# Two cross-attentions in a six-stage kernel: products with values of the preceding batch directly behind the scores, all key and value units behind them

## The chip, the cores and the metric

The kernel runs on one core of a Trainium2 chip. The metric is the device time of one execution in microseconds (us). The median of three runs is 664.64 us (663.59 to 665.05). Names of engines: PE is TensorE (matrix products; PEld is its loading of weights), DVE is VectorE, ACT is ScalarE, POOL is GpSimd, SP is SyncE, which issues the DMAs here.

## The reference, cut to what matters

The input is `x` of 16 batches x 32 tokens x 256 channels, and a context of 16 batches x 512 keys x 256 channels. Six stages follow one another; each adds its result to `x` after a layer norm. Two of them are cross-attentions with 16 heads of 16 channels, and the change is in these:

```python
# stage 1 (L0), x = x + this; _qdq rounds to int8 steps
q = _qdq(layernorm(x)) @ _qdq(wq).T + bq
k, v = split(ctx @ wkv.T + bkv)
attn = softmax(einsum('bnhd,bmhd->bhnm', q, k) / sqrt(16))
out = _qdq(einsum('bhnm,bmhd->bnhd', attn, v)) @ _qdq(wp).T + bp
# stage 4 (L1), x = x + this
scores = where(attend, clip(q @ k / 4, -50, 50), -10000), clipped again
probs = softmax(scores); ctx = probs @ v
delta = layernorm(rs * (ctx @ Wo.T + bo)) * gamma + beta
```

Stages 2 and 5 are self-attentions, stages 3 and 6 feed-forward blocks; nothing in them changes.

## The kernel before, in words

There is no scheduler: each engine's program is written out by hand in its order, and engines wait for one another by semaphores. `xattn` (from L195) writes both cross-attentions, with `L0` true for the first stage. Both run over the 16 batches. What one batch b needs of PE:

- **Scores**: `scores_rows` in stage 1 (L426, 8 products in the program, queries on the partitions), `scores_cols` in stage 4 (L441, 16 products, keys on the partitions). Four banks of PSUM, `S`, take them.
- **Units** of keys and values (`unit_pe`): keys and values of a context batch are four units, two of keys (L388) and two of values (L396). They run some batches ahead of the scores that read them. `slot(b, k)` says which unit stands in which place of batch b: three places a batch, now and then a fourth in stage 1, two from batch 10 on in stage 4, none in the last batch. Units take the two banks `U` in turn; a unit waits until its bank's last unit, two before it, has been copied out. Even units are copied out by ACT (`unit_act`, L674 and L676), odd ones by DVE (`unit_dve`, L685 and L687).
- **Products with values** (`values`, L476, 64 products in the program): they are those of batch b-1, into one of the two banks `O`. In stage 4 they wait for all exponentials of batch b-1 (L561), in stage 1 for the transposed probabilities of b-1, for which the scores of b wait already (L418, L419).
- In stage 1 also **the turn** (`turn`, L451, 16 transposes): the probabilities of batch b are transposed for the next batch. Each quarter waits for its exponential (L694).

The softmax runs on DVE (a maximum in stage 1, L813; a clip in stage 4, L826) and ACT (exponentials, L694 and L700). `take_out` (L714) on ACT copies a batch's products with values out of bank `O`. At the first batch of each four it also waits until `turn_taken` (L493) on PE has read the buffer `oc`.

Every four batches make a tile of 128 tokens, and its end is spread over later batches: `turn_taken` transposes what was taken out (L493), `rows_ready` on DVE divides by the sums (and rounds in stage 1, L860 and L188 to L195), `turn_out` on PE transposes the result (L508 in stage 1, L510 in stage 4), `copy_out_cols` on ACT copies it to SBUF (L723), `out_rows` on PE multiplies by the output weight (L519), and DVE adds it up (L872, L877). `turn_out`, `copy_out_cols` and `out_rows` stand in batches 6, 10 and 14. In stage 4 `turn_taken` stands in batches 5, 9 and 13, in stage 1 in 4, 8 and 12.

What sets the order around the change are four functions: `batch_rows_pe` and `batch_rows_act` in stage 1, `batch_cols_pe` and `batch_cols_act` in stage 4. DVE's, POOL's and SP's programs are not touched. SP loads a context batch when the units of the batch three before it are done (three buffers, L312).

Of the kernel before, what the change touches and what calls it, by code (L numbers as in the profile page):

```python
# [197 lines left out]
def xattn(nc, e, take, sem, L0, d):  # L198
# [68 lines left out]
    TURN, READY, OUT, TAKE, NORM = 0, 1, 2, 2, 3  # L267
    n_weights = 6 if L0 else 10

    def tile_at(b, phase):  # L270

        t = b // 4 - 1
        return t if b % 4 == phase and 0 <= t < NT - 1 else None
# [92 lines left out]
    def slot(b, k):  # L366

        if not L0:
            u = FIRST + 3 * min(b, FULL) + 2 * max(b - FULL, 0) + k
            return None if k >= (3 if b < FULL else 2) or u >= 4 * NB else u  # L370
        u = FIRST + 3 * b + k + max(b - 1, 0) // 4
        return None if (k == 3 and (b % 4 or not b)) or u >= 4 * NB else u

    def unit_pe(pe, u):

        if u is None:
            return
        b, i = u // 4, u % 4
        bank = U[i % 2]
        wait(pe, s_ev[i % 2], 2 * b + i // 2)  # L380
        if i == 0:
            if b == 0:
                pe.wait_ge(s_wk, 16)
            pe.wait_ge(ctx_in[b % CB], 16 * (b // CB + 1))
        x = ctxT[b % CB]
        if i < 2:
            for c in range(NC):
                last = nc.tensor.matmul(bank, wkv[:, c, i * P:(i + 1) * P], x[:, c, :],  # L388
                                        start=(c == 0), stop=(c == NC - 1))
        else:  # L390
            if u == 2:
                pe.wait_ge(s_kv_in, 32)
            for kk in range(2):
                k = 2 * (i - 2) + kk
                for c in range(NC):
                    last = nc.tensor.matmul(bank[:, kk * D:(kk + 1) * D], x[:, c, k * P:(k + 1) * P],  # L396
                                            wkv[:, c, D:2 * D], start=(c == 0), stop=(c == NC - 1))
        last.then_inc(s_unit, 1)
# [97 lines left out]
    def turn_out(pe, t):  # L496

        if t is None:
            return
        pe.wait_ge(s_or, t + 1)  # L500
        if BPT * t + 5 < NB:
            pe.wait_ge(s_o, BPT * t + 5)
        elif after and not L0:
            pe.wait_ge(e.s_yT_out, after.at + t)
        for c in range(NC):
            cols = slice(c * P, (c + 1) * P)
            if L0:
                last = nc.tensor.matmul(OUTB[:, cols], whole[:, t, cols], identb, start=True, stop=True)  # L508
            else:
                last = nc.tensor.transpose(OUTB[:, cols], orow[:, t, cols], e.ident)  # L510
        last.then_inc(s_orT, 1)
# [16 lines left out]
    def batch_rows_pe(pe, b):  # L528

        scores_rows(pe, b)  # L530
        turn_out(pe, tile_at(b, OUT))
        unit_pe(pe, slot(b, 0))
        if b:
            for g in range(G):
                values(pe, b - 1, g)
        out_rows(pe, tile_at(b, TAKE))
        unit_pe(pe, slot(b, 1))
        for g in range(G):
            turn(pe, b, g)
        if b < NB - 1:  # L540
            next_turn(pe, tile_at(b, NORM))
        unit_pe(pe, slot(b, 2))
        turn_taken(pe, tile_at(b, TURN))
        unit_pe(pe, slot(b, 3))

    def batch_cols_pe(pe, b):

        scores_cols(pe, b, 0), scores_cols(pe, b, 1)
        turn_out(pe, tile_at(b, OUT))
        unit_pe(pe, slot(b, 0))  # L550
        turn_taken(pe, tile_at(b - 1, TURN))
        unit_pe(pe, slot(b, 1))
        if b:
            all_values(pe, b - 1)
        out_rows(pe, tile_at(b, TAKE))
        unit_pe(pe, slot(b, 2))
        next_turn(pe, normed(b))
        unit_pe(pe, slot(b, 3))
# [172 lines left out]

    def batch_rows_act(act, b):

        copy_out_cols(act, tile_at(b, OUT))
        exp_rows(act, b, 0), exp_rows(act, b, 1)
        for u in own(b, 0, 0):
            unit_act(act, u)
        exp_rows(act, b, 2), exp_rows(act, b, 3)
        if b:
            take_out(act, b - 1)  # L740
        for u in own(b, 0, 1):
            unit_act(act, u)
        copy_pT_act(act, b, 0), copy_pT_act(act, b, 2)
        if b < NB - 1:
            next_cols(act, tile_at(b, NORM))
        for u in own(b, 0, 2, 3):
            unit_act(act, u)

    def batch_cols_act(act, b):

        copy_out_cols(act, tile_at(b, OUT))
        exp_cols(act, b, 0), exp_cols(act, b, 1)
        for u in own(b, 0, 0):
            unit_act(act, u)
        exp_cols(act, b, 2), exp_cols(act, b, 3)
        for u in own(b, 0, 1):
            unit_act(act, u)
        if b:
            take_out(act, b - 1)
        for u in own(b, 0, 2):  # L760
            unit_act(act, u)
        next_cols(act, normed(b))
        for u in own(b, 0, 3):
            unit_act(act, u)
# [1524 lines left out]
```

## Time and profile before

| | |
|---|---|
| median of 3 runs | 664.64 us (663.59 to 665.05) |
| profiled execution, its own time | 665.43 us |
| its span in the profile | 663.6 us |
| stage 1, batches 0 to 15 | 37.2 us to about 200 us |
| stage 4, batches 0 to 15 | 409.7 us to about 543 us |
| PE busy over the span | 637.4 us (96%) |
| DVE, ACT, POOL busy | 421.4, 274.5, 59.0 us |
| PE's granted clock | 1.00 throughout |

A timeline row gives the start in us from the span's start, the length of the group, the engine, the line, the operation, the shapes and how often; in brackets how long the engine had idled before it, and what ended that. PE's groups overlap a little in these rows, because the ends of products are modelled. The time that a group takes is therefore read from its start to the next group's start. In the trace a product of 32-bit numbers counts as two instructions, so that the 64 products of `values` are 128 there, each with a weight load.

### The profile page before, as it was taken

The page shows a single profiled execution, that of the slowest core. Times are in us where ns is not written, and L with a number is a line of the kernel's source. Part 1 is how long each engine was busy: PE and PEld are TensorE (multiplying, and loading weights), DVE is VectorE, ACT ScalarE, POOL GpSimd, SP SyncE. Part 2 cuts the span into 40 slices and gives each one's busy share as a digit, 9 for nine tenths or more (in the row PEclk, how much of TensorE's full clock was granted, in tenths as well). Part 3 has the DMA queues.
Part 4 walks back from the last instruction along what each step waited for, and adds up shares of the span by engine and source line. Part 5 has one row for each costly group of instructions (what it writes and reads, how often), then busy time and mean ns, then how long its engine had stood idle before and what let it go on. Part 6 is the DMA issues. An engine that isn't in the chain of part 4 may idle for free.

```text
span 663.6 us, 21569 instructions
## 1 busy us (share of the span) xinstructions
PE 637.4 (96%) x9568; PEld 427.7 (64%) x9570; DVE 421.4 (63%) x981; ACT 274.5 (41%) x502; POOL 59.0 (9%) x130
## 2 busy tenths in 40 slices
PE   9999999999988999999999999999999999999976
PEld 4666667567565566666666666777767775466754
DVE  2744468587765656555554773554888965787487
ACT  3454445445442233434333844544454454011134
POOL 1020000001001111011111003000010101000000
PEclk9999999999999999999999999999999999999999
DMA  7241111117005410001003612110182100000001
GB/s 241 65 171 63 35 34 55 44 35 224 2 3 202 149 34 26 16 27 33 2 2 89 210 52 64 34 67 34 60 260 97 67 4 1 3 3 2 3 1 33
DMA packets 28957, 42.25 MB, mean 64 GB/s; under 512 B 6080, under 2 KB 18880, under 8 KB 28352
## 3 DMA queue, kind: packets, MB, share of 16 engines
q1 hardware_dynamic: 28720, 40.60, 19.1%
q8 instruction: 76, 1.25, 0.8%
q10 hardware_dynamic: 144, 0.26, 0.1%
q14 instruction: 17, 0.14, 0.1%
HBM read 40.33 MB, written 0.52 MB: 62 GB/s over the span
## 4 chain that ended last, share of the span: by engine, by line
PE 83%; DVE 11%; issue 2%; ACT 2%; DMA 1%; POOL 0%; SPq 0%; DVEq 0%; ACTq 0%
PE psum L396 16%; PE psum L388 16%; PE psum L1146 7%; PE psum L476 6%; PE psum L441 5%; PE psum L451 4%; PE psum L1197 4%; PE psum L1152 4%; PE psum L1882 2%; PE psum L426 2%; PE psum L1861 2%; PE psum L1167 2%; PE psum L1842 1%; PE psum L1181 1%; DVE arena L1978 1%
## 5 line engine op out<-in xcount | busy, mean ns | idle before, releaser
L396 PE MATMUL psum<-arena 128*128 128x256 f32 x512 | 121.6, 384 | 0.1
L388 PE MATMUL psum<-arena 128*128 128x512 f32 x248 | 117.8, 602 | 0.0
L396 PEld LDWEIGHTS psum<-arena 128*128 128x128 f32 x512 | 93.9, 190 | 22.0 <-issue 9.0
L388 PEld LDWEIGHTS psum<-arena 128*128 128x128 f32 x248 | 43.4, 190 | 41.0 <-issue 39.2
L700 ACT ACTIVATE arena<-arena 128x512 f32<-128x512 f32 x64 | 47.8, 804 | 35.5 <-DVE arena L826 35.5
L694 ACT ACTIVATE arena<-psum,arena 128x512 f32<-128x512 f32 x64 | 40.2, 687 | 31.0 <-DVE arena L813 30.9
L1146 PE MATMUL psum<-y_cols,arena 128*128 128x512 f32 x112 | 52.9, 605 | 0.0
L476 PEld LDWEIGHTS psum<-arena 128*17 128x17 f32 x4096 | 38.5, 96 | 20.1 <-issue 13.0
L826 DVE TENSOR_SCALAR arena<-psum 128x512 f32<-128x512 f32 x64 | 39.7, 681 | 17.9 <-PE psum L441 17.9
L1249 ACT ACTIVATE arena<-psum 128x512 f32<-128x512 f32 x48 | 28.2, 597 | 48.2 <-PE psum L1146 30.9
L813 DVE TENSOR_REDUCE arena<-psum 128x1 f32<-128x512 f32 x64 | 39.7, 683 | 12.8 <-PE psum L426 12.5
L674 ACT ACTIVATE arena<-psum,arena 128x512 f32<-128x512 f32 x42 | 28.8, 685 | 42.5 <-PE psum L388 36.8
L476 PE MATMUL psum<-arena 128*17 128x32 f32 x4096 | 42.7, 197 | 3.0 <-issue 2.9
L676 ACT ACTIVATE arena<-psum 128x512 f32<-128x512 f32 x42 | 25.1, 598 | 41.2 <-PE psum L396 41.2
L1303 DVE TENSOR_REDUCE arena<-psum 128x8 f32<-128x256 f32 x16 | 6.8, 425 | 48.1 <-PE psum L1167 48.1
L441 PEld LDWEIGHTS psum<-arena 64*128 64x128 f32 x512 | 29.9, 188 | 6.6 <-issue 6.1
L326 POOL TENSOR_TENSOR arena<-arena,head_mask 128x64 f32<-128x64 f32 (+1 forms) x64 | 20.7, 349 | 147.2 <-PE psum L426 92.1
L441 PE MATMUL psum<-arena 64*128 64x128 f32 x512 | 32.9, 278 | 0.0
L451 PEld LDWEIGHTS psum<-ident,arena 128*128 128x128 f32 x256 | 28.8, 141 | 6.0 <-issue 3.5
L1146 PEld LDWEIGHTS psum<-y_cols,arena 128*128 128x128 f32 x112 | 20.1, 189 | 18.6 <-issue 17.8
L451 PE MATMUL psum<-ident,arena 128*128 128x128 f32 x256 | 30.8, 273 | 1.2 <-ACT arena L694 1.2
L1152 PE MATMUL psum<-arena,y_cols 128*128 128x256 f32 x128 | 31.9, 392 | 0.0
(249 smaller groups left out, 932.7 us busy)
## 6 DMA issues: line engine op xcount, KB each, us to landing
arena<-in_ctxT SPq DMA_DIRECT2D x31, 512.0 KB, 3.7
arena<-in_L_attn_Wv SPq DMA_DIRECT2D x1, 2048.0 KB, 8.3
arena<-in_L_attn_Wq SPq DMA_DIRECT2D x8, 256.0 KB, 3.0
arena<-in_L_attn_Wk SPq DMA_DIRECT2D x8, 256.0 KB, 3.6
arena<-in_L_attn_Wo SPq DMA_DIRECT2D x1, 2048.0 KB, 12.3
arena<-in_L_ffn_w_gating SPq DMA_DIRECT2D x1, 2048.0 KB, 7.8
arena<-in_wo_rows SPq DMA_DIRECT2D x2, 1024.0 KB, 5.1
arena<-in_wq_upT SPq DMA_DIRECT2D x2, 768.0 KB, 7.7
```

The source lines that it names most:

```text
L388: last = nc.tensor.matmul(bank, wkv[:, c, i * P:(i + 1) * P], x[:, c, :], start=(c == 0), stop=(c == NC - 1))
L396: last = nc.tensor.matmul(bank[:, kk * D:(kk + 1) * D], x[:, c, k * P:(k + 1) * P], wkv[:, c, D:2 * D], start=(c == 0), stop=(c == NC - 1))
L441: ins = nc.tensor.matmul(S[2 * kp + r][:, (2 * kk + h) * P:(2 * kk + h + 1) * P], kT[home(b)][a, h, k * P:(k + 1) * P], qbd[b % QBUFS][a, ...
L451: last = nc.tensor.transpose(S[g][:, k * P:(k + 1) * P], pr[g][:, k * P:(k + 1) * P], e.ident)
L476: last = nc.tensor.matmul(O[b % 2][j * SQ:j * SQ + VW, g * SQ:(g + 1) * SQ], va[home(b)][:, k, head, :], probs[:, j * SQ:(j + 1) * SQ], st ...
L674: ins = nc.scalar.activation(kT[home(b)][:, i, :], U[i % 2], ACT.Identity, bias=bk[:, i:i + 1])
L694: nc.scalar.activation(pr[g], S[g], ACT.Exp, bias=nmx[:, g:g + 1]).then_inc(s_exp, 1)
L700: nc.scalar.activation(pTk[b % 2][k], clip[k // 2][:, k % 2, :], ACT.Exp, bias=mb[:, b, k:k + 1], scale=m01[:, b, k:k + 1]).then_inc(s_exp, 1)
L813: nc.vector.tensor_reduce(nmx[:, g:g + 1], S[g], AX.X, ALU.max, negate=True).then_inc(s_mx, 1)
L826: nc.vector.tensor_scalar(dst, S[i].rearrange("p (a n) -> p a n", n=P), 50.0, -50.0, ALU.min, ALU.max)\
L1146: last = nc.tensor.matmul(bank, w[:, c, f], e.yT[:, c, :], start=(c == 0), stop=(c == NC - 1))
L1152: last = nc.tensor.matmul(bank[:, (t % 2) * 2 * DV:(t % 2 + 1) * 2 * DV], e.yT[:, c, t * P:(t + 1) * P], wv[:, c, p * 2 * DV:(p + 1) * 2 * ...
```

## The change: the diff, and what it moves

In both stages the products with values of batch b-1 move up on PE, directly behind the scores of batch b, ahead of `turn_out` and of all units of the batch. On ACT, `take_out` moves up to follow them, between the first two and the last two exponentials; `copy_out_cols` moves from the head of the batch to behind it; and the copy of the batch's first unit moves behind the last two exponentials. The first batch has no products with values, so its order on PE stays, but ACT's changes there too. No instruction is added or removed.

```diff
--- before.py
+++ after.py
@@ -528,11 +528,11 @@
     def batch_rows_pe(pe, b):
 
         scores_rows(pe, b)
-        turn_out(pe, tile_at(b, OUT))
-        unit_pe(pe, slot(b, 0))
         if b:
             for g in range(G):
                 values(pe, b - 1, g)
+        turn_out(pe, tile_at(b, OUT))
+        unit_pe(pe, slot(b, 0))
         out_rows(pe, tile_at(b, TAKE))
         unit_pe(pe, slot(b, 1))
         for g in range(G):
@@ -546,12 +546,12 @@
     def batch_cols_pe(pe, b):
 
         scores_cols(pe, b, 0), scores_cols(pe, b, 1)
+        if b:
+            all_values(pe, b - 1)
         turn_out(pe, tile_at(b, OUT))
         unit_pe(pe, slot(b, 0))
         turn_taken(pe, tile_at(b - 1, TURN))
         unit_pe(pe, slot(b, 1))
-        if b:
-            all_values(pe, b - 1)
         out_rows(pe, tile_at(b, TAKE))
         unit_pe(pe, slot(b, 2))
         next_turn(pe, normed(b))
@@ -731,13 +731,13 @@
 
     def batch_rows_act(act, b):
 
+        exp_rows(act, b, 0), exp_rows(act, b, 1)
+        if b:
+            take_out(act, b - 1)
         copy_out_cols(act, tile_at(b, OUT))
-        exp_rows(act, b, 0), exp_rows(act, b, 1)
+        exp_rows(act, b, 2), exp_rows(act, b, 3)
         for u in own(b, 0, 0):
             unit_act(act, u)
-        exp_rows(act, b, 2), exp_rows(act, b, 3)
-        if b:
-            take_out(act, b - 1)
         for u in own(b, 0, 1):
             unit_act(act, u)
         copy_pT_act(act, b, 0), copy_pT_act(act, b, 2)
@@ -748,15 +748,15 @@
 
     def batch_cols_act(act, b):
 
+        exp_cols(act, b, 0), exp_cols(act, b, 1)
+        if b:
+            take_out(act, b - 1)
         copy_out_cols(act, tile_at(b, OUT))
-        exp_cols(act, b, 0), exp_cols(act, b, 1)
+        exp_cols(act, b, 2), exp_cols(act, b, 3)
         for u in own(b, 0, 0):
             unit_act(act, u)
-        exp_cols(act, b, 2), exp_cols(act, b, 3)
         for u in own(b, 0, 1):
             unit_act(act, u)
-        if b:
-            take_out(act, b - 1)
         for u in own(b, 0, 2):
             unit_act(act, u)
         next_cols(act, normed(b))
```

PE, stage 1, from the scores of batch 5 (first row) over those of batch 6 (seventh row) to the middle of batch 6, before (L388 and L396 units, L476 products with values of the batch before, L451 the turn, L508 `turn_out`, L519 `out_rows`):

```order
L426 MATMUL psum<-arena 64x512 x8
L388 MATMUL psum<-arena 128x512 x2
L476 MATMUL psum<-arena 17x32 x64
L388 MATMUL psum<-arena 128x512 x2
L451 MATMUL psum<-ident,arena 128x128 x16
L396 MATMUL psum<-arena 128x256 x4
L426 MATMUL psum<-arena 64x512 x8
L508 MATMUL psum<-arena 128x128 x2
L396 MATMUL psum<-arena 128x256 x4
L476 MATMUL psum<-arena 17x32 x64
L519 MATMUL psum<-arena 128x256 x2
L388 MATMUL psum<-arena 128x512 x2
```

The same stretch in the changed kernel:

```order
L426 MATMUL psum<-arena 64x512 x8
L476 MATMUL psum<-arena 17x32 x64
L388 MATMUL psum<-arena 128x512 x4
L451 MATMUL psum<-ident,arena 128x128 x16
L396 MATMUL psum<-arena 128x256 x4
L426 MATMUL psum<-arena 64x512 x8
L476 MATMUL psum<-arena 17x32 x64
L508 MATMUL psum<-arena 128x128 x2
L396 MATMUL psum<-arena 128x256 x4
L519 MATMUL psum<-arena 128x256 x2
L388 MATMUL psum<-arena 128x512 x2
L451 MATMUL psum<-ident,arena 128x128 x16
```

L476 now stands behind L426 in both batches, the unit that stood between them has joined the next unit (a unit of keys is two of L388, a unit of values four of L396; L388 x4 is two units), and in batch 6 L508 has the products with values ahead of it.

ACT, stage 1, batch 10 before, from its first instruction (L723 `copy_out_cols`, L694 exponentials, L674 copy of a unit, L714 `take_out`, L706 copies of the turn):

```order
L723 ACTIVATE arena<-psum 128x256
L694 ACTIVATE arena<-psum,arena 128x512 x2
L674 ACTIVATE arena<-psum,arena 128x512
L694 ACTIVATE arena<-psum,arena 128x512 x2
L714 ACTIVATE arena<-psum 128x4x32
L706 ACTIVATE arena<-psum 128x512 x2
```

The same batch in the changed kernel:

```order
L694 ACTIVATE arena<-psum,arena 128x512 x2
L714 ACTIVATE arena<-psum 128x4x32
L723 ACTIVATE arena<-psum 128x256
L694 ACTIVATE arena<-psum,arena 128x512 x2
L674 ACTIVATE arena<-psum,arena 128x512
L706 ACTIVATE arena<-psum 128x512 x2
```

L723 has moved from the head to behind two exponentials and L714; L674 stands behind the last exponential.

ACT, stage 4, batch 0 before, with the head of batch 1 behind it (L700 exponentials, L674 and L676 copies of units):

```order
L700 ACT_TABLE_LOAD
L700 ACTIVATE arena<-arena 128x512 x2
L674 ACTIVATE arena<-psum,arena 128x512
L700 ACTIVATE arena<-arena 128x512 x2
L676 ACTIVATE arena<-psum 128x32x16
L700 ACTIVATE arena<-arena 128x512 x4
```

And in the changed kernel:

```order
L700 ACT_TABLE_LOAD
L700 ACTIVATE arena<-arena 128x512 x4
L674 ACTIVATE arena<-psum,arena 128x512
L676 ACTIVATE arena<-psum 128x32x16
L700 ACTIVATE arena<-arena 128x512 x2
L714 ACTIVATE arena<-psum 128x4x32
```

The copy of the first unit (L674) has moved behind all four exponentials, and in batch 1 L714 stands between them.

## Rows read from the trace of the kernel before

**Rows 1.** The page: busy time and count by engine; the queue that carries instructions.

```profile
PE 637.4 (96%) x9568; PEld 427.7 (64%) x9570; DVE 421.4 (63%) x981; ACT 274.5 (41%) x502; POOL 59.0 (9%) x130
...
q8 instruction: 76, 1.25, 0.8%
```

**Rows 2.** Busy time by stretch: start:end length, then each engine's busy time; clock, DMA share.

```profile
37.20:190.10 152.90, 150.53 (x2590) 100.27 (x2589) 100.05 (x194) 74.36 (x134) 8.81 (x31) 1.00 0.22 72
409.70:545.00 135.30, 134.99 (x2867) 99.72 (x2867) 96.66 (x190) 67.95 (x114) 15.72 (x38) 1.00 0.26 80
```

**Rows 3.** Timeline of PE, first stage, one batch: start, length, instructions; in brackets idle before.

```profile
64.54 1.11 PE L426 MATMUL psum<-arena 32*64 32x512 f32 x16
65.58 1.99 PE L388 MATMUL psum<-arena 128*128 128x512 f32 x4
67.50 1.32 PE L476 MATMUL psum<-arena 128*17 128x32 f32 x128
68.75 1.99 PE L396 MATMUL psum<-arena 128*128 128x256 f32 x8
```

**Rows 4.** Timeline of PE, fourth stage, one batch.

```profile
434.59 2.06 PE L441 MATMUL psum<-arena 64*128 64x128 f32 x32
436.58 1.98 PE L388 MATMUL psum<-arena 128*128 128x512 f32 x4
438.40 1.89 PE L396 MATMUL psum<-arena 128*128 128x256 f32 x8
440.22 1.32 PE L476 MATMUL psum<-arena 128*17 128x32 f32 x128
441.47 1.99 PE L396 MATMUL psum<-arena 128*128 128x256 f32 x8
443.39 0.83 PE L441 MATMUL psum<-arena 64*128 64x128 f32 x10
```

**Rows 5.** Timeline of PE, fourth stage, last batch.

```profile
536.29 2.06 PE L441 MATMUL psum<-arena 64*128 64x128 f32 x32
538.28 1.32 PE L476 MATMUL psum<-arena 128*17 128x32 f32 x128
539.52 0.66 PE L1796 MATMUL psum<-arena 128*128 128x64 f32 x4
```

**Rows 6.** Timeline of PE, first stage, where a token tile is taken.

```profile
98.59 0.28 PE L508 MATMUL psum<-arena 128*128 128x128 bf16 x2 [0.29 <-DVEq L862]
```

**Rows 7.** Timeline of PE and ACT, first stage, batch 10.

```profile
138.56 1.11 PE L426 MATMUL psum<-arena 32*64 32x512 f32 x16
...
140.28 0.38 ACT L723 ACTIVATE arena<-psum 128x256 bf16<-128x256 f32 x1 [3.19 <-PE psum L508]
...
141.69 1.29 ACT L694 ACTIVATE arena<-psum,arena 128x512 f32<-128x512 f32 x2 [1.02 <-DVE arena L813]
...
144.58 0.30 ACT L714 ACTIVATE arena<-psum 128x128 f32<-128x128 f32 x1
```

**Rows 8.** Timeline of ACT and PE, fourth stage, batch 0.

```profile
412.17 1.52 ACT L700 ACTIVATE arena<-arena 128x512 f32<-128x512 f32 x2 [0.51 <-DVE arena L826]
...
415.19 1.89 PE L396 MATMUL psum<-arena 128*128 128x256 f32 x8
```

**Rows 9.** Timeline of PE and ACT, fourth stage, batch 8.

```profile
480.05 2.06 PE L441 MATMUL psum<-arena 64*128 64x128 f32 x32
...
483.17 1.52 ACT L700 ACTIVATE arena<-arena 128x512 f32<-128x512 f32 x2 [4.62 <-DVE arena L826]
...
484.60 0.67 ACT L674 ACTIVATE arena<-psum,arena 128x512 f32<-128x512 f32 x1
```

**Rows 10.** Timeline of PE, idle times inside or behind products with values.

```profile
77.11 1.19 PE L476 MATMUL psum<-arena 128*17 128x32 f32 x112
79.79 0.31 PE L476 MATMUL psum<-arena 128*17 128x32 f32 x16 [1.50 <-issue]
...
194.29 1.53 PE L451 MATMUL psum<-ident,arena 128*128 128x128 f32 x12 [0.95 <-ACT arena L694]
```

## Prediction

> **What bounds the kernel now.** I read the page first. PE is busy 637.4 of 663.6 us [rows 1], and the chain that ended last runs over PE for most of the span. The table by stretch then says what idle time is left in the two cross-attentions: 152.90 less 150.53 us, so 2.4 us, in stage 1 (ending before its last batch), and 0.3 us in stage 4 [rows 2]. So the change can't gain by filling idle time. It can gain only if PE's own work takes less time in another order, and it loses by every wait that it brings. The granted clock is 1.00 in both stretches [rows 2], the higher of the two levels (2.4 GHz), and PE has no pause to lose it in, so I leave the clock out.
>
> **What an order costs PE.** The timeline of one batch, read from start to start, shows that the same work takes different times by its neighbours. In stage 4 the first unit of the batch takes 1.82 us (436.58 to 438.40), the second 1.82, the third 1.92 (441.47 to 443.39) [rows 4]. The first has the scores before it, the second the products with values behind it, the third has both kinds of neighbour. So a side on which a unit meets scores or products with values costs 0.10 us, and a bare unit is 1.72. Stage 1 agrees: its first unit stands between scores and products with values and takes 1.92 (65.58 to 67.50) [rows 3]. I call such a side a border. Products with values take 1.25 us between two units (440.22 to 441.47) [rows 4]. In the last batch of stage 4 no unit stands between: scores 1.99 (536.29 to 538.28), products 1.24 (538.28 to 539.52) [rows 5], the same as with units around. So where scores meet products with values directly, nothing is seen to be paid.
>
> **Part 1, fewer borders.** A full batch has four borders before (scores to unit, unit to products, products to unit, unit to scores) and two after (products to unit, unit to scores): 2 x 0.095 = 0.19 us less, taking 0.095 for the border between these roundings. Stage 1 has 11 such batches (1 to 14 without 6, 10, 14): 2.1 us. Stage 4 has 8 (1 to 5, 7 to 9): 1.5. Batch 6 and batches 10 to 14 of stage 4 have other neighbours (an output product behind the products with values, or scores directly behind them); they save one border or less, 0.5 us together. Sum 4.1 us. Bounds: from below 2.1, if scores meeting products cost a border that the last batch doesn't show; from above no more than the 4.1.
>
> **Part 2, the wait of `turn_out` in stage 1.** In batches 6, 10 and 14 PE idles 0.29 us ahead of L508 [rows 6], since DVE has not finished rounding. After the change 1.25 us of products stand ahead of it, so DVE is long done. With one border less in each, 3 x (0.29 + 0.10) = 1.2 us. Next late there is `out_rows`, priced in part 3. From below the gain is nothing, from above 1.2.
>
> **Part 3, what ACT is late with.** ACT has idle time on average (its busy times in [rows 2] are half the stretches), so the moved instructions cost nothing by themselves; the copies of units and of `turn_out` are now behind exponentials, and these wait for DVE. I laid each batch out with the start-to-start times above. In a full batch of stage 4 PE's third unit, in the bank of the first, starts 1.99 + 1.25 + 1.82 + 1.72 = 6.78 us behind the start of the scores. ACT copies that first unit in even batches.
> - Stage 4, batch 0, has no products with values, and PE's order there is unchanged: its third unit starts at 415.19, right behind the second. ACT's exponentials start at 412.17, late behind a table load. Two of them hold ACT 1.43 us (483.17 to 484.60), a copy lasts 0.67 [rows 8, 9]. All four exponentials and then the copy: 412.17 + 2.86 + 0.67 = 415.70. PE waits 0.5 us.
> - Stage 4, batch 8: DVE is behind, so the exponentials start 3.12 us after the scores [rows 9], and 0.19 later by this measure once batch 7 is shorter. 3.31 + 1.43 + 0.20 for `take_out` (its 0.30 [rows 7] overlaps its neighbours) + 1.43 + 0.67 = 7.04, against 6.78. PE waits 0.3 us. In the other even batches the exponentials start 0.6 us earlier and the copy is there with 0.3 to 0.5 us to spare.
> - Stage 1, batch 10: the maxima on DVE are late, because rounding and a unit's copy stand ahead of them; the exponentials start at 141.69, 3.13 us behind the scores at 138.56 [rows 7]. Before, `copy_out_cols` stood ahead of them (140.28). Now it follows two exponentials (1.29) and `take_out`: 141.69 + 1.20 + 0.20 + 0.38 = 143.5. `out_rows` on PE is due at 138.56 + 1.04 for the scores [rows 3] + 1.25 + 0.28 for L508 [rows 6] + 1.72 = 142.85. PE waits 0.7 us. In batches 6 and 14 the exponentials start 0.9 us sooner, and 0.2 us are to spare.
> - The last batch of stage 4 has `take_out` amid its exponentials, ahead of the last products: 0.1 us.
>
> Together 1.6 us. In batches 5, 9 and 13 of stage 4 `take_out` waits for `turn_taken`, which now comes 1.25 us later on PE; behind it queue the last two exponentials and a copy, which nobody needs before the next batch. DVE's order is unchanged; it gets the first unit 1.25 us later, copies it in 0.7 and has it ready 0.9 us before its bank is wanted. POOL and SP wait for scores and for units done, and these keep their rhythm; no DMA is issued in another order. Bounds of part 3: 0.5 us, if only batch 0 slips; about 4 us, if every even batch of stage 4 loses 0.3 and batches 6 and 14 do too.
>
> **Part 4, instructions that arrive late.** Two waits of PE can't be explained by any engine: 1.50 us inside the products with values from 78.30 on, and 0.95 us from 193.34 on, behind them (the exponential named was over by then) [rows 10]. A third like them stands at the end of stage 1. PE and its weight loads are 19,138 instructions, brought by 76 packets of 1.25 MB in sum [rows 1], so a packet brings about 250. The products with values are 256 of them in 1.25 us; a whole batch has some 350 to 400. So about every batch some packet has to come within a short time, and the second wait stands at the one place of stage 1 where products directly follow scores. That is the order that all batches now get: scores and products are 290 to 320 instructions in 2.3 to 3.2 us, where before a unit or two lay between. What that costs no row shows for the new order. From below: -1.5, if the wait at 78.30 goes; from above: four waits more at about 1.3, 5.2 us. I take one more wait net of what may go, 1.5 us, near the rows that are there.
>
> **Sum.** 4.1 + 1.2 - 1.6 - 1.5 = 2.2 us less than the profiled execution's own 665.43: 663.2. That execution lies 0.8 us above the median 664.64, so the forecast is 662.5 us, 0.33% less. What a measurement of this kernel can tell from no change is about 0.2%, 1.3 us.
>
> The Trainium skill, page "TensorEngine Tiling (Array Packing)", section "Tiling Modes", says that a change of tiling mode drains TensorE. The units use the whole array, scores and products with values two different tilings (the shapes 64*128 and 128*17 in the rows), so by the rule scores meeting products is a change of mode as well, and a batch goes from four changes to three, not to two. The row of the last batch speaks against a price for this one; by the rule it would have one, and that is the second rival.
>
> **The rivals.**
> 1. Better than the forecast: no new instruction waits, and the one at 78.30 goes. 4.1 + 1.2 - 1.6 + 1.5 = 5.2 us, so 659.4. For it: such waits are rare in the trace before, three in 30 batches. Against it: the denser order.
> 2. Scores to products costs a border. One border less per batch, not two: 28 x 0.095 = 2.7 us less gain, but no less loss. 662.5 + 2.7 less what rounding leaves = 665.1, no change. For it: every other meeting of kinds costs 0.10. Against it: 1.24 us in [rows 5].
> 3. ACT slips at every even batch of stage 4: part 3 at 4 us instead of 1.6. 664.9, no change. For it: the margins of 0.2 to 0.5 us are small against semaphore times, which I have not counted one by one.
> 4. Slower: late instruction packets. The mechanism is that of part 4, its place the products with values behind the scores, its price 1.3 us each. It decides from about three more waits than before (4.1 + 1.2 - 1.6 = 3.7 us); with four, 4.1 + 1.2 - 1.6 - 5.2 = -1.5, so 666.1.
> 5. That the change doesn't do what it says: the order of instructions shows that it does.
>
> **Chances.** Forecast 45%, rival 1 18%, rival 2 12%, rival 3 10%, rival 4 15%. Of the forecast's 45 points 8 fall within 0.2%. Rivals 2 and 3 fall within it too, but for 2 points each on the slow side: 8 + 10 + 8 = 26 same; 37 + 18 = 55 faster; 15 + 2 + 2 = 19 slower. The range reaches nearly from rival 1 to rival 4, 659.6 to 666.0.
>
> **What would show it.** Right: in the timeline of PE a batch of stage 1 takes 9.4 us and not 9.60, one of stage 4 8.6 and not 8.80; products with values still 1.25; no wait ahead of L508; a wait ahead of L519 in batch 10 of stage 1 that ACT L723 ends; a wait ahead of the third unit in batches 0 and 8 of stage 4 that ACT L674 ends. Wrong: products with values of 1.35 us behind scores (rival 2); waits at L396 or L388 in most even batches of stage 4 (rival 3); idle times of about 1 us inside or just behind L476 that no engine ends (rival 4), or none at all (rival 1).

## The result and the profile after

The changed kernel takes 668.48 us (median of 5 runs, 668.07 to 670.22) against 664.64 (663.59 to 665.10) before: 1.0062 times the time, 95% interval 1.0046 to 1.0078. It is slower by 3.8 us. The forecast was 2.1 us faster, and the time lies outside its range. Rival 4 came true, at a greater size than it was given, and a second loss joined it that no part of the prediction had priced.

The profiled execution took 670.22 us, with a span of 668.4, so it is one of the slower ones; the one before took 665.43 with a span of 663.6. First the busy time of the page, and the two cross-attentions in the table by stretch (columns as in [rows 1, 2]):

```profile
PE 637.3 (95%) x9568; PEld 431.3 (65%) x9570; DVE 421.2 (63%) x981; ACT 272.0 (41%) x502; POOL 59.2 (9%) x130
```

```profile
36.60:193.70 157.10, 150.70 (x2597) 102.52 (x2604) 100.47 (x195) 73.23 (x134) 8.96 (x31) 0.99 0.22 70
413.60:550.00 136.40, 133.50 (x2866) 100.12 (x2866) 96.09 (x188) 65.98 (x112) 15.77 (x38) 1.00 0.25 80
```

PE's busy time in the whole kernel is what it was. But in stage 1, from the first batch's scores to the last's, PE now idles 157.10 - 150.70 = 6.4 us where it idled 2.4, in stage 4 2.9 us where it idled 0.3, and the granted clock of stage 1 has gone from 1.00 to 0.99 [rows 2]. Who ends PE's idle time is told by the table of waits (us in total, times, longest); of its eleven rows these four concern the two stages:

```profile
PE psum L476 <- issue: 7.8, 6, 2.4
PE psum L396 <- issue: 1.6, 3, 0.9
...
PE psum L519 <- ACT arena L723: 1.0, 2, 0.5
...
PE psum L451 <- ACT arena L694: 0.8, 2, 0.6
```

"issue" is a wait that no engine, semaphore or data transfer ends. The row of L476 alone was 2.9 us before and is 7.8 now. Now the steps of the prediction. The timeline of PE, one plain batch of stage 1, answers to [rows 3]:

```profile
44.70 1.11 PE L426 MATMUL psum<-arena 32*64 32x512 f32 x16
45.75 1.34 PE L476 MATMUL psum<-arena 128*17 128x32 f32 x128
47.02 1.99 PE L396 MATMUL psum<-arena 128*128 128x256 f32 x8
48.85 1.88 PE L388 MATMUL psum<-arena 128*128 128x512 f32 x4
50.57 1.91 PE L451 MATMUL psum<-ident,arena 128*128 128x128 f32 x16
52.32 1.89 PE L388 MATMUL psum<-arena 128*128 128x512 f32 x4
54.13 1.11 PE L426 MATMUL psum<-arena 32*64 32x512 f32 x16
```

54.13 - 44.70 = 9.43 us, where a batch took 9.60. The products with values take 1.27 behind the scores. One of stage 4, which answers to [rows 4]:

```profile
439.90 2.06 PE L441 MATMUL psum<-arena 64*128 64x128 f32 x32
441.88 1.32 PE L476 MATMUL psum<-arena 128*17 128x32 f32 x128
443.13 1.98 PE L388 MATMUL psum<-arena 128*128 128x512 f32 x4
444.95 3.62 PE L396 MATMUL psum<-arena 128*128 128x256 f32 x16
448.50 0.38 PE L441 MATMUL psum<-arena 64*128 64x128 f32 x2
```

448.50 - 439.90 = 8.60, where it took 8.80. So the borders were saved in both stages. The waits of parts 2 and 3, from the same view, in batch 10 of stage 1 and batches 0 and 8 of stage 4:

```profile
143.50 0.29 PE L508 MATMUL psum<-arena 128*128 128x128 bf16 x2
...
146.09 0.39 PE L519 MATMUL psum<-arena 128*128 128x256 bf16 x2 [0.52 <-ACT arena L723]
...
419.69 1.99 PE L396 MATMUL psum<-arena 128*128 128x256 f32 x8 [0.39 <-ACT arena L674]
...
491.58 1.99 PE L396 MATMUL psum<-arena 128*128 128x256 f32 x8 [0.28 <-ACT arena L674]
```

No wait stands ahead of L508 any more [rows 6], and all three waits on ACT are where they were forecast. And now what went wrong, in batch 4 of stage 1:

```profile
74.47 1.11 PE L426 MATMUL psum<-arena 32*64 32x512 f32 x16
75.51 1.25 PE L476 MATMUL psum<-arena 128*17 128x32 f32 x117
79.11 0.29 PE L476 MATMUL psum<-arena 128*17 128x32 f32 x11 [2.35 <-issue]
79.34 5.40 PE L388 MATMUL psum<-arena 128*128 128x512 f32 x8
84.58 1.91 PE L451 MATMUL psum<-ident,arena 128*128 128x128 f32 x16
```

Two losses stand here one behind the other. After 117 of the 128 products PE stops for 2.35 us; in the same batch it stopped for 1.50 before, there after 112 of them [rows 10]. Then eight L388, which take 3.54 us in a run shown further below, take 5.24 (79.34 to 84.58). The table by stretch (length, PE busy, clock, DMA share, GB/s) says why:

```profile
78.00:80.00 2.00, 0.89 (x13) 1.00 0.04 14
80.00:82.00 2.00, 2.00 (x5) 0.62 0.03 8
82.00:84.00 2.00, 2.00 (x4) 0.52 0.00 0
84.00:86.00 2.00, 2.00 (x16) 1.00 0.00 0
```

The granted clock falls to about a half (1.2 GHz of 2.4) after the pause and comes back to 1.00 at 84. From its scores to those of batch 5, batch 4 takes 15.84 us where it took 13.45 before. The same pair, waits at 197.46 and 201.68 and then a clock of 0.50 in 204 to 206, stands at the stage's end. Behind these waits, before and after:

```profile
199.70 2.82 PE L1125 MATMUL psum<-y_cols,arena 128*128 128x384 f32 x8
202.91 0.28 PE L508 MATMUL psum<-arena 128*128 128x128 bf16 x2 [0.39 <-DVEq L862]
...
203.02 4.51 PE L1125 MATMUL psum<-y_cols,arena 128*128 128x384 f32 x8
207.37 0.28 PE L508 MATMUL psum<-arena 128*128 128x128 bf16 x2
```

The eight L1125 and the wait of 0.39 ahead of L508 took 3.21 us together before; now the eight alone take 4.35 (203.02 to 207.37) and the wait is gone, 1.1 us more.

**What ends the waits.** The DMA rows show it. The stretch of 55 to 59 us, in 40 slices of 0.1 us, holds two transfers and nothing else, both of the queue that carries instructions; PE's wait beside it is from the timeline:

```profile
GB/s 0 164 0 0 0 0 0 0 0 0 0 0 0 0 0 0 0 0 0 0 0 0 0 0 0 0 0 0 0 0 0 0 0 0 0 0 164 0 0 0
DMA packets 2, 0.03 MB, mean 8 GB/s; under 512 B 0, under 2 KB 0, under 8 KB 0
...
q8 instruction: 2, 0.03, 2.9%
```

```profile
55.18 1.06 PE L476 MATMUL psum<-arena 128*17 128x32 f32 x97
57.56 0.33 PE L476 MATMUL psum<-arena 128*17 128x32 f32 x19 [1.31 <-issue]
```

One packet of 16 KB starts in the second slice, at 55.2, and by its record has landed at 56.12; PE goes on at 57.56, 1.4 us later. I counted PE's records to each wait that no engine ends in the two stages, and subtracted the landing of the last packet before it. The count takes in products, weight loads and also the 282 instructions of PE that compute nothing (280 for semaphores, two drains), which the timeline leaves out; with products and weight loads alone, 938, 1698, 2454 and so on, nothing regular shows:

```
changed kernel, record   960  1728  2496  5056  5824  6080 10944 13504 14528 15296
= 256 k + 192, k =         3     6     9    19    22    23    42    52    56    59
PE goes on at, us       57.6  79.1 103.5 176.5 197.5 201.7 434.4 498.2 521.9 537.9
idle, us                1.32  2.35  0.86  1.34  0.65  1.56  0.92  0.54  0.33  0.21
after the landing, us   1.43  1.41  1.37  1.41  1.35  1.37  1.36  1.41  1.36  1.26
before, record                1728                    5824  6080
idle, us                      1.50                    0.95  1.40
```

All ten stand, to within one record, at the same place of the 256 instructions that a packet brings, and all ten end 1.3 to 1.4 us after a packet has landed. The size fits: the queue's 76 packets [rows 1] for 19,420 records are one per 256. And if the packets and the places 256 k + 192 are paired one to one in their order, PE passes no such place sooner than 1.17 us after its packet landed, in any of the profiled runs of this document; in the two stages of the changed kernel the ten waits have 1.26 to 1.43 us, and of the places without a listed wait one has 1.34 us and all others 1.86 or more. They are 8.1 us in stage 1 (3.9 before) and 2.0 us in stage 4 (none before). From here on I call them late packets. (The one of 0.65 us is put down to ACT by the timeline, as its like was before [rows 10]; the count shows that it belongs here.)

### The profile page after: what moved, and what is told of

Same layout as the page of the kernel before. It is cut to its first block, busy times and chain, and to the rows that moved or that the text cites. A ratio compares the mean times of both kernels' runs of the same rounds, so it can differ in the third digit from the quotient of the medians.

```text
span 668.4 us, 21569 instructions
## 1 busy us (share of the span) xinstructions
PE 637.3 (95%) x9568; PEld 431.3 (65%) x9570; DVE 421.2 (63%) x981; ACT 272.0 (41%) x502; POOL 59.2 (9%) x130
## 3 DMA queue, kind: packets, MB, share of 16 engines
q8 instruction: 76, 1.25, 0.7%
## 4 chain that ended last, share of the span: by engine, by line
PE 82%; DVE 11%; issue 3%; ACT 3%; POOL 0%; DVEq 0%; ACTq 0%; POOLq 0%
PE psum L396 16%; PE psum L388 15%; PE psum L1146 7%; PE psum L476 5%; PE psum L451 4%; PE psum L441 4%; PE psum L1197 4%; PE psum L1152 4%; PE psum L426 2%; PE psum L1882 2%; PE psum L1167 2%; PE psum L1861 2%; PE psum L1842 1%; PE psum L1181 1%; DVE arena L1978 1%
## 5 line engine op out<-in xcount | busy, mean ns | idle before, releaser
L396 PE MATMUL psum<-arena 128*128 128x256 f32 x512 | 120.4, 382 | 2.3 <-issue 1.6
L388 PE MATMUL psum<-arena 128*128 128x512 f32 x248 | 117.8, 606 | 0.0
L396 PEld LDWEIGHTS psum<-arena 128*128 128x128 f32 x512 | 94.4, 190 | 24.1 <-issue 9.0
L388 PEld LDWEIGHTS psum<-arena 128*128 128x128 f32 x248 | 44.6, 192 | 40.0 <-issue 38.6
L700 ACT ACTIVATE arena<-arena 128x512 f32<-128x512 f32 x64 | 48.4, 806 | 45.8 <-DVE arena L826 41.3
L694 ACT ACTIVATE arena<-psum,arena 128x512 f32<-128x512 f32 x64 | 40.8, 691 | 37.3 <-DVE arena L813 37.3
L476 PEld LDWEIGHTS psum<-arena 128*17 128x17 f32 x4096 | 39.1, 96 | 22.1 <-issue 19.8
L476 PE MATMUL psum<-arena 128*17 128x32 f32 x4096 | 43.7, 197 | 7.8 <-issue 7.8
L674 ACT ACTIVATE arena<-psum,arena 128x512 f32<-128x512 f32 x42 | 28.8, 686 | 45.6 <-PE psum L388 40.4
L676 ACT ACTIVATE arena<-psum 128x512 f32<-128x512 f32 x42 | 25.1, 597 | 46.2 <-PE psum L396 46.2
L687 DVE COPY arena<-psum 128x512 f32<-128x512 f32 x22 | 15.2, 691 | 29.5 <-PE psum L396 28.9
L685 DVE TENSOR_SCALAR arena<-psum,arena 128x512 f32<-128x512 f32 x22 | 16.5, 750 | 26.8 <-PE psum L388 26.6
L451 PEld LDWEIGHTS psum<-ident,arena 128*128 128x128 f32 x256 | 28.8, 141 | 5.8 <-issue 3.8
```

Of the source, the lines that this page charges most:

```text
L451: last = nc.tensor.transpose(S[g][:, k * P:(k + 1) * P], pr[g][:, k * P:(k + 1) * P], e.ident)
L476: last = nc.tensor.matmul(O[b % 2][j * SQ:j * SQ + VW, g * SQ:(g + 1) * SQ], va[home(b)][:, k, head, :], probs[:, j * SQ:(j + 1) * SQ], st ...
L674: ins = nc.scalar.activation(kT[home(b)][:, i, :], U[i % 2], ACT.Identity, bias=bk[:, i:i + 1])
L694: nc.scalar.activation(pr[g], S[g], ACT.Exp, bias=nmx[:, g:g + 1]).then_inc(s_exp, 1)
L700: nc.scalar.activation(pTk[b % 2][k], clip[k // 2][:, k % 2, :], ACT.Exp, bias=mb[:, b, k:k + 1], scale=m01[:, b, k:k + 1]).then_inc(s_exp, 1)
```

## The experiments

Kernels measured together ran on one chip beside the kernel before, and each ratio is against that; times of kernels measured apart are compared across chips. The theory in all of them: the run of scores and products with values, 144 small products in stage 1 without anything between, uses instructions up faster than packets bring them.

**Half of the products with values left out, in both orders.** Key tiles 2 and 3 are not multiplied, so the output is not the reference's.

```diff
-        for k in range(KT):
+        for k in range(2):
             probs = pT[g][:, k, :] ...
```

> The kernel before, with half of the products with values left out (two of four key tiles), so that these are 128 instructions of PE in 0.62 us instead of 256 in 1.25. It is the yardstick for the next kernel. Both theories: about 32 x 0.62 = 20 us less than before, 645 us. Late packets of instructions: at most two waits of PE that no engine ends are left.

> The changed kernel with the same half of the products with values left out. Theory (late packets of instructions: scores and products with values back to back outrun them): with 128 instructions fewer per batch the packets keep up, the waits are gone or nearly so, and what is left of the change is the gain by fewer borders and turn_out less ACT's waits, 3 to 4 us: 641 to 643 us, faster than the half kernel before. Rival (the order itself costs, by ACT's late copies or by the meeting of scores and products): still about 4 us slower than the half kernel before, 649 us.

Old order 647.69 us (ratio 0.9728, 0.9714 to 0.9742), new order 645.72 (0.9707, 0.9691 to 0.9723). With half the small products there is no late packet in either stage of either kernel, and the new order is no longer 3.8 us slower but about 2 us faster in the medians of four runs each; the two intervals overlap a little, and both times lie 2.7 us above what I had expected. In the profiled executions the borders are saved (8.87 us a batch of stage 1 against 9.04, 8.04 against 8.23 in stage 4), but the new order waits longer for ScalarE (1.09 us ahead of L519 in batch 10, 1.22 ahead of L396 in batch 8 of stage 4), and its span is the longer one, 644.1 against 643.6. So the loss goes with the late packets; whether the whole saving of 3.7 us is there the run doesn't show.

**The packets' edges moved.** n small products at the very start move every edge by 4 n instructions against the batches.

```diff
+            for _ in range(n):     # n = 16, 32, 48
+                nc.tensor.matmul(e.B[5][0:17, 0:32], e.neghalf[:, 0:1].to_broadcast([P, 17]),
+                                 e.neghalf[:, 0:1].to_broadcast([P, 32]), start=True, stop=True)
```

> The changed kernel with 32 small products at the very start, while PE waits for the first DMA: 128 more instructions of PE, so that every packet of instructions ends half a packet earlier in the program; all else is the same. Theory: the waits that no engine ends move to other batches and change in number and length, and the time moves by 1 us or more, either way (666 to 671 or, if the places are lucky, 662 to 666). Rival: the same 668.5 within 0.7 us, with the waits in the same batches.

> The kernel before with the same 32 small products at its start. It is the control: they cost nothing in themselves (PE waits there for the first DMA). Theory: the waits at 78.30, 193.34 and 196.95 us move or go and new ones may come, 662 to 667 us. Rival: 664.6 within 0.7 us.

> The old order with 16 one-pass products of 17x32 put in at the very start, 64 instructions on TensorE, which move every packet's edge by 64 against the batches; output unchanged. Theory (where the edges fall against the runs of small products decides how many packets are late): the waits that no engine ends stand at other batches, still at 192 of 256 counted with the added ones, and the time lies anywhere from 661 to 675 us, about 1 us of it for the start. Rival (the shift by 128 was slow for another reason, its own cost at the start): 665.5 to 666.5 us, the old time and half of the start's cost.

> The changed kernel with the same 64 instructions at the start. Theory (the new order, in which a run is of 144 small products, meets a packet's edge more often, whatever the shift): 2 to 6 us above the old order with the same shift. Rival (the order is neutral and the alignment a matter of luck): within 2 us of it, or below.

> The old order with 48 such products, 192 instructions. Theory: waits at yet other batches, at 192 of 256, 661 to 675 us. Rival (a cost of the added products themselves): it grows with their number, 1.5 times what 32 cost, near 679 us.

> The changed kernel with the same 192 instructions. Theory: 2 to 6 us above the old order with the same shift, by more waits that no engine ends. Rival: within 2 us of it, or below.

```
moved by   old order, us (ratio)                  new order, us (ratio)
   0       664.64                                 668.48 (1.0062, 1.0046 to 1.0078)
  64       666.45 (1.0018, 1.0003 to 1.0034)      668.54 (1.0047, 1.0028 to 1.0066)
 128       674.54 (1.0141, 1.0106 to 1.0176)      678.14 (1.0182, 1.0168 to 1.0196)
 192       668.93 (1.0052, 1.0035 to 1.0070)      675.36 (1.0157, 1.0131 to 1.0183)
late packets in the profiled runs, stage 1 / stage 4, us
   0       3.9 / 0                                8.1 / 2.0
  64       3.4 / 0                                8.0 / 0
 128       2.8 / 2.3                              8.6 / 3.7
 192       1.7 / 0.2                              8.6 / 1.9
first scores of stage 1 in the profiled runs, us
   0       37.2                                   36.5
  64       37.8                                   37.3
 128       38.1                                   38.8
 192       39.3                                   39.7
```

Both kernels move by up to 10 us, and the waits stand at count 192 of 256 again, the added products counted. Moved by 128, both came out 7 us above the range that I had expected. With the added products the first scores come 0.6 to 2.1 us later in the old order and 0.8 to 3.1 in the new one, part of it scatter (without them they lie between 36.1 and 37.3 in the profiled runs). The rest of the 10 us is not the cost of the added products: 48 of them cost the old order less than 32. At each of the four alignments the new order is slower, by 2.1 to 6.4 us (at 64 and 128 the intervals overlap a little); it isn't the luck of one. Its late packets of stage 1 are 8.0 to 8.6 us at every alignment, the old order's 1.7 to 3.9. In the slow 128 case of the old order the profile shows 8.2 us of late packets in the whole kernel, 3.7 more than at 0, 0.9 us at the start, and three places with a clock of 0.5, from 164.2, 212.0 and 580.7 us on, of 3.4 us each, where there was none at 0. One such stretch cost 1.7 us above (5.24 less 3.54), so three may cost 5.1: 3.7 + 0.9 + 5.1 = 9.7, an upper bound, where the profiled execution is 8.4 us longer and the median 9.9.

The worst place of all is in the new order moved by 192, batch 12 of stage 1:

```profile
161.37 0.94 PE L476 MATMUL psum<-arena 128*17 128x32 f32 x83
167.09 0.83 PE L476 MATMUL psum<-arena 128*17 128x32 f32 x45 [4.79 <-issue]
167.85 5.98 PE L396 MATMUL psum<-arena 128*128 128x256 f32 x16
173.67 1.91 PE L451 MATMUL psum<-ident,arena 128*128 128x128 f32 x16
```

4.79 us of waiting, and then sixteen L396, which take 3.6 us elsewhere, take 5.82: this one packet costs 7 us.

**One stage at a time.** The diff in stage 1 alone (`batch_rows_pe`, `batch_rows_act`), and in stage 4 alone (`batch_cols_pe`, `batch_cols_act`).

> The new order in stage 1 alone; stage 4 has the old one. Theory (late instruction packets and the clock's drop behind them): stage 1 ends 3 to 4 us later than before, by the same waits at the same counts of TensorE instructions (192 in 256) as in the changed kernel, and stage 4 runs as before: 667 to 668.5 us. Rival (the loss is ScalarE's new order, which is late in both stages): stage 1 alone costs under 1.5 us, 664.5 to 666.

> The new order in stage 4 alone. Theory (late packets): four waits that no engine ends, 2 us together, less 3 us of borders, 0.9 us of waits on ScalarE and later transfers: 665 to 666.5 us, which is 1.5 us above before as between the two landmarks of the traces. Rival (the stage 4 waits follow from the delay that stage 1 hands on, through the phase of the transfers): without it they are gone and stage 4 gains its borders, 662 to 663.5 us.

Stage 1 alone: 669.14 us (1.0060, 1.0045 to 1.0074); the same six late packets in stage 1 (8.6 us) and one of 0.7 in stage 4. Stage 4 alone: 667.04 (1.0031, 1.0017 to 1.0045); stage 1 as before, 2.4 us late in stage 4, at three of the four counts of the changed kernel. So each stage loses by itself. Both came out somewhat above what I had expected, and their sum is more than the loss of the two together; the clock adds its part in some runs and not in others (stage 4 alone: nine runs with a mean clock of 1.00 took 664.9 to 667.6, three with 0.994 or 0.995 took 669.1 to 669.3).

**TensorE's part alone.** `batch_rows_act` and `batch_cols_act` as before.

> TensorE's new order in both stages with ScalarE's old one. Theory (the loss sits in TensorE's instruction supply): the same waits at the same counts, 667 to 670 us. Rival (ScalarE's part of the change is what costs): 662 to 664.6 us.

670.38 us (1.0073, 1.0061 to 1.0085), just above the 667 to 670 expected and not faster than the full change. In the two stages 10.3 us of late packets, about as with the change. The table of waits of stage 4 (409 to 560 us):

```profile
PE psum L476 <- issue: 1.8, 2, 1.6
PE psum L396 <- issue: 1.3, 2, 0.7
PE psum L158 <- DVE y_rows L142: 0.2, 1, 0.2
```

No wait on ACT is left there, and none ahead of L519 in batches 6, 10 and 14 of stage 1 either. ScalarE's part of the change brought only the 1.2 us of waits of part 3. In the medians that gain doesn't show.

**Half of the products behind the scores, half behind the first unit.** ScalarE as before.

```diff
+        if b:
+            values(pe, b - 1, 0), values(pe, b - 1, 1)
         turn_out(pe, tile_at(b, OUT))
         unit_pe(pe, slot(b, 0))
         if b:
-            for g in range(G):
-                values(pe, b - 1, g)
+            values(pe, b - 1, 2), values(pe, b - 1, 3)
```

> ScalarE as before; on TensorE two of the four groups of products with values stand directly behind the scores and two behind the batch's first unit, in both stages, so that the 128 small products never stand together. Theory (a packet is late because 128 to 144 small instructions are used up within 1.3 to 2.4 us): the waits that no engine ends go from 3.9 us before to under 1 us, the wait ahead of the turned outputs goes too (0.9 us), borders are as many as before: 659.5 to 662 us. Rival (the waits come from where the packets' edges fall and come elsewhere when the order is changed, or the transfers of other queues make them late): 663.5 to 668 us, with as many such waits as before or after.

666.12 us (1.0017, 1.0007 to 1.0028), not the 659.5 to 662 expected. The profiled run has 2.9 us late in stage 1 and nothing in stage 4, less than before, but a batch takes 9.71 us, 0.11 more than before. I had counted as many borders as before, but each half of the products has edges of its own. This run doesn't separate the theories.

**Half behind the scores, half behind the turned probabilities, stage 1 only.** `take_out` on ScalarE goes behind the copies of units.

```diff
+        if b:
+            values(pe, b - 1, 0), values(pe, b - 1, 1)
         turn_out(pe, tile_at(b, OUT))
         unit_pe(pe, slot(b, 0))
-        if b:
-            for g in range(G):
-                values(pe, b - 1, g)
...
             turn(pe, b, g)
+        if b:
+            values(pe, b - 1, 2), values(pe, b - 1, 3)
```

> Stage 4 as before. In stage 1 two groups of the products with values stand behind the scores and two behind the batch's turned probabilities, so the borders between kinds of products are as few as in the changed kernel, but no run of small products is longer than 80. Theory (the long run makes packets late): the waits that no engine ends stay at or below the 3.9 us of before, borders give 1.5 us and the wait ahead of the turned outputs 0.9: 661 to 664 us. Rival (any new order of stage 1 has more late packets): 666 to 670 us.

> The same with 64 instructions added at the start. Theory: no slower than the old order with the same shift (666.5 us), 663 to 667 us. Rival: 668 to 672 us, as the changed kernel with it or worse.

> The same with 128 instructions added. Theory: no slower than the old order with the same shift (674.5 us), 664 to 675 us. Rival: 676 to 680 us.

> The same with 192 instructions added. Theory: no slower than the old order with the same shift (668.9 us), 664 to 669 us. Rival: 671 to 677 us.

At the four alignments 665.65 us (0.9998, 0.9985 to 1.0011), 664.64 (0.9986, 0.9972 to 1.0000), 673.95 (1.0130, 1.0112 to 1.0149) and 667.96 (1.0038, 1.0023 to 1.0052). Late packets of stage 1: 1.8, 0.3, 0 and 0 us, where the changed kernel has 8.1, 8.0, 8.6 and 8.6. At alignment 0 it can't be told from the old order; at the other three it is 0.6 to 1.8 us below it (the intervals lie apart at 64 alone), and at all four 2.8 to 7.4 us below the changed kernel. This is the test of the theory, and for stage 1 it holds: with the same products and no run over 80, nearly all packets of stage 1 come in time at the four alignments tried. What is left at 128 lies elsewhere: 3.87 us at L1168 in stage 2 and 2.6 us in stage 4. The borders were again misjudged (a batch takes 9.70, not 9.4); so the first time was above the 661 to 664 us expected.

**The short runs in stage 1, the changed order in stage 4, ScalarE as in the runs above.**

> Stage 1 as in split_turns, stage 4 with the changed kernel's order on TensorE and the old one on ScalarE. Theory: stage 4 saves 2.0 us at its borders and pays 1.5 to 3 us of late packets, as in the changed kernel at this alignment, where they stand at the same counts: 665 to 667 us, no gain on split_turns (665.65). Rival (with ScalarE's old order stage 4 gains): 663 to 664.5 us.

> The same with 64 instructions added at the start, where the changed kernel with the same shift has no late packet in stage 4. Theory: the borders show in full, 2.0 us less than split_turns_pad16 (664.64): 662 to 663.5 us, faster than both kernels. Rival (stage 4's order costs something else that hid behind the packets): 664.5 us or more.

664.91 us (1.0000, 0.9986 to 1.0013), at the lower end of the theory's range, and moved by 64, where stage 4 has no late packet, 661.92 (0.9956, 0.9942 to 0.9971). The second is faster than both kernels, by 0.44% of the former and, across chips, about 1.0% of the latter. Its stage 1 around the place of the 2.35 us wait:

```profile
74.93 1.11 PE L426 MATMUL psum<-arena 32*64 32x512 f32 x16
75.97 0.76 PE L476 MATMUL psum<-arena 128*17 128x32 f32 x64
76.66 3.71 PE L388 MATMUL psum<-arena 128*128 128x512 f32 x8
80.20 1.91 PE L451 MATMUL psum<-ident,arena 128*128 128x128 f32 x16
82.04 0.73 PE L476 MATMUL psum<-arena 128*17 128x32 f32 x64
82.71 1.99 PE L396 MATMUL psum<-arena 128*128 128x256 f32 x8
```

Nothing waits here, and the eight L388 take 3.54 us, not 5.24; one late packet is left in stage 1, at its end, of 0.8 us in the first kernel and 0.9 in the second. In stage 4 of the second a batch has the changed kernel's order and no wait. Its time is 2.7 us below the same kernel with stage 4 as before (664.64), where 2.0 was expected. So the saved borders of stage 4 do show in the time once the packets are there.

## Why the prediction was wrong

**Part 1, fewer borders: held.** 9.43 and 8.60 us a batch against 9.4 and 8.6; the products took 1.27 and 1.25. Rival 2 is out: a border between scores and products would have been 0.10. The Trainium skill, page "TensorEngine Tiling (Array Packing)", section "Tiling Modes", says that a change of mode drains TensorE; the trace shows 0.02 us or less for this one.

**Part 2, `turn_out`: held.** No wait ahead of L508 in any of the three batches.

**Part 3, ScalarE: held in place, and nearly in size.** 0.52 + 0.39 + 0.28 = 1.2 us, forecast 1.6. Rival 3 is out. What I didn't ask was whether this part was needed at all; the run with ScalarE's old order has none of these waits.

**Part 4, late packets: this step failed.** It took "one more wait net of what may go, 1.5 us", and gave the upper bound as four more, 5.2 us. In the profiled execution it was seven more, and 10.1 us instead of 3.9 in the two stages: 6.2 us. Two things were wrong in it. The price of one, 1.3 us, was if anything too high (the ten have a mean of 1.0), and the bound of four more had no reason of its own: I took the waits as rare events of the trace (three in 30 batches) when the argument beside it, 290 to 320 instructions in 2.3 to 3.2 us and a packet of some 250, gave a mechanism for every batch in which a packet's edge falls into the run. And I let the low end reach below nothing "if the wait at 78.30 goes"; it grew to 2.35.

**The clock: left out, wrongly.** "PE has no pause to lose it in" was true of the trace before and not of the kernel that part 4 describes. Two stretches at half clock cost about 1.7 + 1.1 = 2.8 us in the profiled execution (the second 1.5, less the wait of 0.39 that it took in). The page "TensorE: Matmul & The Clock Gate" of the Trainium skill, Part 1, has the clock halve when the engine has been idle and come back when it is busy; the rows at 80 to 84 us agree, at 0.62 and 0.52. But the length of one pause doesn't decide it here: in the changed kernel moved by 64, a wait of 2.70 us ending at 145.45 was followed by a clock of 1.00.

**The sum, by the profiled executions.** -4.1 (borders) - 1.2 (L508) + 1.2 (ACT) + 6.2 (late packets) + 2.8 (clock) = +4.9 us; the spans differ by 668.4 - 663.6 = 4.8. That the two agree so closely is in part luck. From its first scores to its last rows, stage 1 grew by 4.5 us (from the scores of batch 0 to the L1125 of 208.97 before, 212.81 now) and stage 4 by 1.6, together 6.0: a wait takes 0.15 to 0.18 us more from the batch than its idle time, which the sum leaves out. Outside the two stages the profiled execution was faster: its first scores came 0.6 us earlier, within the scatter of the runs, and a late packet of stage 6 cost 0.2 us instead of 0.6.

**What stays open.** Why a packet starts so late. I timed each packet's start, in the kernel before and the changed one, from record 256 k + 144 of PE, 304 records ahead of the place it serves. Where the packet before it was usable for PE by then, about two thirds start 0.6 to 1.6 us after that record, the others up to 6.1. Where it wasn't, as behind a run of small products, the packet starts 1.2 to 8.4 us after it; the packet of 55.2 us is the one of 8.4. That is read from two traces, not tested. Open is also when the clock falls, and with it part of the time at 128 and 192. Open too is the part of the medians: an unprofiled run of the changed kernel at a clock of 1.00 took 668.21 us, 3.6 above the median before, where the account without the clock gives 2.1. The waits may differ from run to run; only profiled runs show them.

## What to carry to other kernels

When the profile shows waits on TensorE that no engine ends, count its instructions between them, those that only wait for semaphores too: if the distance is a multiple of 256, the instruction supply is a resource like any other, and in this kernel long runs of small products are what exhausted it. Before two such runs are joined to save an edge of 0.1 us, price the packet that falls between them, here 0.2 to 4.8 us a piece and the clock behind it; two short runs a few microseconds apart cost less here. A kernel that is near this limit should be compared at several alignments, since 64 to 192 instructions more at the start moved this one by up to 10 us, more than the change of this document.

## What the hardware showed that I had not expected

- A packet of 16 KB serves 256 instructions of TensorE; each of the ten late ones was missed at the same count, 192 of 256, and PE went on 1.3 to 1.4 us after its landing. The Trainium skill, page "Runtime: NRT & Kernel Launch", section "Instruction fetch mechanics", gives the 256 instructions a block and calls the cost of crossing one mostly hidden. The trace agrees on the size; here it was 10.1 us in the two stages.
- 64, 128 or 192 small instructions at the start moved the old order by +1.8, +9.9 and +4.3 us against 664.64; in the profiled runs 0.6, 0.9 and 2.1 of it were there before stage 1.
- A pause of 2.35 us in busy TensorE work was followed by 3.4 us at half clock, from 80.5 us on; in the kernel before, one of 1.50 in the same batch was not (batch 4 took 13.45 us, 1.50 + 0.18 above the 11.77 of batches 8 and 12, which have the same work and no wait), nor one of 2.70 in the changed kernel moved by 64.
- A half of the run of 128 products costs 0.66 to 0.69 us, both together 1.35, where the whole costs 1.25.
